# A two-block transformer-like kernel on one core: one softplus in the attention, squares on two engines, value products of four heads together, loops written out

## The reference, cut to what matters

```python
# attention: 16 heads of size 16, 1024 tokens, 4 sequences
scores = jnp.einsum('bhqd,bhkd->bhqk', q, k) * hs ** (-0.5)
p = jax.nn.softplus(scores)
p = p * p
p = p * causal
attn = p / (jnp.sum(p, axis=-1, keepdims=True) + 1e-09)
out = jnp.einsum('bhqk,bhkd->bhqd', attn, v)
...
# experts: 8, the two with the largest gate
gates = jax.nn.softmax(jnp.einsum('bsh,eh->bse', x, gate_w) + gate_b, axis=-1)
top_gates, top_idx = jax.lax.top_k(gates, TOP_K)
expert_out = jnp.einsum('bsh,eoh->bseo', x, expert_w) + expert_b
selected = jnp.take_along_axis(expert_out, top_idx[..., None], axis=2)
return (selected * top_gates[..., None]).sum(axis=2)
```

## Time and profile before

| | us |
|---|---|
| median of 3 runs | 1797.35 |
| lowest, highest | 1796.25, 1797.80 |
| span of the profiled execution, first to last instruction | 1794.8 |
| what lies around the span (median less span) | 2.55 |
| ACT busy over the whole span | 1092.9 (61%) |
| POOL busy over the whole span | 858.2 (48%) |

### The profile page before, as it was taken

How to read it: one execution, slowest core, us unless ns; L and a number is a source line. 1 busy time by engine, 2 the same in 40 slices (tenths; PEclk the granted TensorE clock), 3 DMA queues, 4 the chain that set the end, 5 groups by cost and what they waited for, 6 DMA issues and landing times. The chain is left out here.

```text
span 1794.8 us, 33269 instructions
## 1 busy us (share of the span) xinstructions
PE 1683.5 (94%) x11188; PEld 1158.1 (65%) x11188; DVE 1295.7 (72%) x2830; ACT 1092.9 (61%) x1612; POOL 858.2 (48%) x654
## 2 busy tenths in 40 slices
PE   8999897999999999998999899998899999889999
PEld 7888773333333333338788777777677777667777
DVE  5455885777777777775545788886787787778886
ACT  3332788999999999993333322214888887722120
POOL 0002108999999999995003322211265665411111
PEclk9999998999999999999999999999999999999999
DMA  5000275635535535400000100001232233200000
GB/s 164 1 0 12 91 214 90 76 48 73 68 47 73 67 47 79 62 1 1 13 1 30 29 7 0 0 0 39 83 96 95 104 112 103 95 1 24 23 23 24
DMA packets 57112, 95.09 MB, mean 53 GB/s; under 512 B 7904, under 2 KB 29632, under 8 KB 57024
## 3 DMA queue, kind: packets, MB, share of 16 engines
q1 hardware_dynamic: 56064, 93.35, 24.0%
q10 hardware_dynamic: 960, 0.59, 0.1%
HBM read 76.88 MB, written 17.04 MB: 52 GB/s over the span
## 5 line engine op out<-in xcount | busy, mean ns | idle before, releaser
L1508 POOL TENSOR_TENSOR att_weights<-att_weights 128x1024 f32<-128x1024 f32 (+1 forms) x288 | 508.9, 1799 | 9.0 <-DVE att_weights L1445 5.6
L1445 DVE SCALAR_TENSOR_TENSOR att_weights<-att_weights,ps 128x512 f32<-128x512 f32 x544 | 348.2, 684 | 145.1 <-ACT att_weights L1414 138.6
L932 DVE SCALAR_TENSOR_TENSOR X<-ps,moe_gsel,X 128x256 f32 (+1 forms) x512 | 246.6, 484 | 63.1 <-PE ps L48 44.8
L1369 PE MATMUL ps<-att_weights,att_v_ones 64*32 64x64 f32 (+5 forms) x2048 | 289.0, 399 | 1.9 <-POOL att_weights L1508 1.8
L1414 ACT ACTIVATE att_weights<-att_weights 128x1024 f32<-128x1024 f32 (+1 forms) x288 | 286.5, 1007 | 1.0
L1408 ACT ACTIVATE att_weights<-ps 128x1024 f32<-128x1024 f32 (+1 forms) x288 | 278.4, 972 | 8.6 <-PE ps L1349 7.0
L48 PE MATMUL ps<-w_experts_hi,moe_xh 128*128 128x512 f32 x512 | 205.3, 401 | 0.4 <-DVE X L932 0.4
L48 PE MATMUL ps<-w_experts_hi,moe_xl 128*128 128x512 f32 x512 | 203.2, 397 | 0.0
L48 PE MATMUL ps<-w_experts_lo,moe_xh 128*128 128x512 f32 x512 | 201.6, 394 | 0.0
L1369 PEld LDWEIGHTS ps<-att_weights,att_v_ones 128*32 128x32 f32 (+1 forms) x2048 | 82.4, 108 | 104.6 <-issue 80.2
L424 ACT ACTIVATE ffn_gates<-ps,ffn_gate_bias 128x512 f32<-128x512 f32 x72 | 49.5, 688 | 147.5 <-PE ps L48 143.2
(11 more groups left out here) (282 smaller groups left out, 3796.3 us busy)
## 6 DMA issues: line engine op xcount, KB each, us to landing
ssm_lb<-decays SPq DMA_DIRECT2D x32, 512.0 KB, 4.7
ssm_rise<-decays SPq DMA_DIRECT2D x28, 512.0 KB, 3.9
qk_parts<-qkv_part SPq DMA_DIRECT2D x32, 384.0 KB, 2.7
q_stack<-qk_parts SPq DMA_DIRECT2D x64, 128.0 KB, 4.9
k_stack<-qk_parts SPq DMA_DIRECT2D x64, 128.0 KB, 8.4
att_q_stack<-qk_parts SPq DMA_DIRECT2D x64, 128.0 KB, 4.7
att_k_stack<-qk_parts SPq DMA_DIRECT2D x64, 128.0 KB, 8.5
out<-X SPq DMA_DIRECT2D x7, 512.0 KB, 2.9
```

What stands on the lines that cost most here:

```text
L932: dve.scalar_tensor_tensor(out=x, in0=ring[:, e // 2, (e % 2) * C:(e % 2 + 1) * C], scalar=gsel[:, s, j, e:e + 1], in1=x, op0=ALU.mult, op ...
L1369: ins = pe.matmul(O(qb)[h * 2 * HD:(h + 1) * 2 * HD, q0:q0 + w], values, Wt[rows, u % WU, t, c:c + w], start=kj == 0 and part == FULL, sto ...
L1445: dve.scalar_tensor_tensor(out=wt[:, t], in0=wt[:, t], scalar=LIMIT, in1=scores(u)[:, t], op0=ALU.min, op1=ALU.max).then_inc(max_done, 2 // n)
L1508: pool.tensor_tensor(wt, wt, wt, ALU.mult).then_inc(sq_pool, 1)
```

## The change

In the attention ACT runs one `Softplus` from PSUM to SBUF in place of `Exp` and `Ln`, and DVE's min and max are gone; a score place is free when softplus has read it. The squares are split: POOL squares seven of a pass's 18 units (0, 2, 6, 8, 10, 12, 14; all wide), DVE the other eleven (nine wide, two narrow). Both operands of DVE's square lie in SBUF. The value products of a step (two units, four heads) are issued together after the second unit's square. AHEAD becomes 6 and the lags become shorter. In `choose`, `max_index` and the comparisons give way to `match_replace`: the two largest are replaced by zero in a copy, and `gsel` is half the difference. The index table and its DMA go. All `Fori` loops become Python loops, so the instructions stand written out.

```diff
-    AHEAD = 7
-    TURN_LAG, COPY_LAG, DEN_LAG, OUT_LAG = 4, 7, 9, 10
+    AHEAD = 6
+    TURN_LAG, COPY_LAG, DEN_LAG, OUT_LAG = 3, 5, 8, 9
...
+    POOL_UNITS = [u for u in range(PU) if BANKS[u] == 2 and u % 2 == 0][:7]
+    by_pool = lambda u: u % PU in POOL_UNITS
...
                 upper = segments[0][-1] == UPPER
+                pe.wait_ge(softplus_done, i * NU + u + 1)
...
-            def value_unit(i, u):
+            def value_step(i, u):
...
+                for unit in range(first, last + 1):
+                    squares_of(i, s * PU + unit)
...
-            act.preload_act_table_set(LN_EXP_SET)
+            act.preload_act_table_set(SOFTPLUS_SET)
...
-                act.activation(Wt[:, u % WU, 0:n], scores(u)[:, 0:n], ACT.Exp).then_inc(exp_done, 1)
+                act.activation(Wt[:, u % WU, 0:n], scores(u)[:, 0:n], ACT.Softplus).then_inc(softplus_done, 1)
...
-                act.activation(wt, wt, ACT.Ln, bias=1.0).then_inc(ln_done, 1)
...
-                    dve.scalar_tensor_tensor(out=wt[:, t], in0=wt[:, t], scalar=LIMIT, in1=scores(u)[:, t],
-                                             op0=ALU.min, op1=ALU.max).then_inc(max_done, 2 // n)
+                dve.wait_ge(softplus_done, SU + i * NU + u + 1)
+                wt = Wt[:, u % WU, 0:BANKS[u % PU]]
+                dve.tensor_tensor(wt, wt, wt, ALU.mult).then_inc(sq_dve, 1)
...
-                    pool.wait_ge(max_done, 2 * (SU + i * NU + u + 1))
-                    wt = Wt[:, u % WU, 0:BANKS[u % PU]]
-                    pool.tensor_tensor(wt, wt, wt, ALU.mult).then_inc(sq_pool, 1)
+                    if by_pool(u):
+                        pool.wait_ge(softplus_done, SU + i * NU + u + 1)
+                        wt = Wt[:, u % WU]
+                        pool.tensor_tensor(wt, wt, wt, ALU.mult).then_inc(sq_pool, 1)
...
+                dve.tensor_copy(taken[:, :, 0:2], best[:, :, 0:2]).then_inc(taken_done, 1)
+                dve.wait_ge(taken_done, n + 1)
                 for j in range(GT):
-                    ins = dve.max_index(place[:, j], best[:, j], prob[:, j])
...
+                    ins = dve.match_replace(rest[:, j], taken[:, j], prob[:, j], 0.0)
...
-            with pe.Fori(1, BODIES - 1) as i:
+            for i in range(1, BODIES - 1):
                 body(i)
```

More of the change, by code:

```diff
@@ L397, in _ @@
             step(0, first=True)
-            with pe.Fori(1, B - 1) as i:
+            for i in range(1, B - 1):
                 step(i)
@@ L433, in _ @@
             step(0, first=True)
-            with act.Fori(1, B - 1) as i:
+            for i in range(1, B - 1):
                 step(i)
@@ L512, in _ @@
             step(0, first=True)
-            with dve.Fori(1, B - 1) as i:
+            for i in range(1, B - 1):
                 step(i)
@@ L527, in _ @@
             norm.pool_rstd(pool, 1, 1)
-            with pool.Fori(1, GROUPS // 2) as i:
+            for i in range(1, GROUPS // 2):
                 for s in range(2):
@@ L805, in _ @@
             group(0, 0)
-            with pe.Fori(0, GROUPS // 2 - 1) as i:
+            for i in range(0, GROUPS // 2 - 1):
                 group(i * 2 + 1, 1)
@@ L868, in _ @@
             apply(1, 1)
-            with act.Fori(0, GROUPS // 2 - 1) as i:
+            for i in range(0, GROUPS // 2 - 1):
                 group(i * 2, 0)
@@ L1016, in _ @@
             split.split(pool)
-            with pool.Fori(0, GROUPS // 2 - 2) as i:
+            for i in range(0, GROUPS // 2 - 2):
                 group(i * 2, 0)
@@ L1087, in steps @@
             step(1, 0, 1, 3)
-            with eng.Fori(1, B - 2) as i:
+            for i in range(1, B - 2):
                 step(i * 2, i, 0, 3)
@@ L1213, in _ @@
             norm.pool_shift(pool, 1, 1)
-            with pool.Fori(0, GROUPS // 2 - 1) as i:
+            for i in range(0, GROUPS // 2 - 1):
                 for h in range(HALVES):
@@ L1514, in _ @@
             copy_v(0, 0, 0)
-            with pool.Fori(0, BODIES - 1) as i:
+            for i in range(0, BODIES - 1):
                 body(i)
@@ L1521, in _ @@
             load_stacks(sp, stacks, loaded, parts_dram, 0, 1, STACKED)
-            with sp.Fori(1, BODIES) as i:
+            for i in range(1, BODIES):
                 for s in range(2):
@@ L1559, in _ @@
             copy_in(0, 1)
-            with act.Fori(0, B - 1) as i:
+            for i in range(0, B - 1):
                 for h in range(HALVES):
@@ L1595, in _ @@
             project(1, 1)
-            with pe.Fori(1, GROUPS // 2 - 1) as i:
+            for i in range(1, GROUPS // 2 - 1):
                 turn_in(i * 2 + 1, 1)
@@ L1622, in _ @@
             lo(0, 0)
-            with dve.Fori(0, GROUPS // 2 - 2) as i:
+            for i in range(0, GROUPS // 2 - 2):
                 lo(i * 2 + 1, 1)
@@ L1733, in groups @@
             group(0, 0, 2)
-            with eng.Fori(0, PT // 2 - 2) as i:
+            for i in range(0, PT // 2 - 2):
                 group(i * 2 + 1, 1, 2)
@@ L2255, in _ @@
             spread(0, 0)
-            with sp.Fori(0, PT // 2 - 1) as i:
+            for i in range(0, PT // 2 - 1):
                 spread(i * 2 + 1, 1)
```

135 lines of the change are left out of this document (55 added, 80 removed).

## The result

The changed kernel takes **1651.7 us** in the median (1648.1 to 1652.8), the kernel before 1796.8 in the same session: a ratio of **0.919, 95% interval [0.918, 0.920]**, 145 us less. The prediction was 1661. The profiled execution took 1652.15 us with a span of 1650.3.

The account below looks back on a forecast made before the run. Bound now: ScalarE, GpSimd close behind; afterwards their shared VectorE-GpSimd port, 47.6 + 2, called 50 us a body. Eight bodies 400 + 9 = 409 against 541.5, with 3.5 more 136 us less: 1661 us, range 1640 to 1696 (8 in 10: 1620 to 1705).

Parts of the forecast that it names:

- ACT: ScalarE in an attention body: one softplus per unit, assumed to cost what `Exp` costs, 32 us.
- A dear softplus: Rival: attention slower than before because softplus is expensive; at 3.0 us a wide unit 2070 us in all; chance 0.03.
- PE: TensorE in an attention body: scores, value products, transposes, 41 us; as rival limit 1589 us in all, wholly or partly 0.12.
- unjoined heads: Rival in the attention's value products: four heads not running together, 56 us a body, 1709 us; 0.10 shared with dearer hand-overs.
- DVE and POOL alone: Attention body, each engine's own work without hindrance: VectorE 29 us, GpSimd 28 us.
- The port: VectorE's two-SBUF-input squares and GpSimd's instructions exclude each other in the attention: 47.6 us a body; chance 0.75 (47.6 to 54).
- The gaps: Attention body: 2 us added because the port won't be full, making 49.6, called 50 us; bounds 47.6 and 54.
- Start, end, clock: Attention outside its eight bodies: 6 us for start and end, 3 us for the half clock (bounds 0 and 8).
- The rest: Savings beside the attention's main sum: expert picking -0.5 us and written-out loops -3 us, together 3.5 us.
- Loops alone: Written-out loops: 0.2 us per group in the state-space layer, -3 us for all stages (bounds -6 and +3).
- the picking: `choose`, picking the experts: a few instructions fewer, hidden behind TensorE except in the first group, -0.5 us.
- Signs: New profile: VectorE's wide squares about 2 us, GpSimd's above 1.89, TensorE waiting for `att_oT` or squares, ScalarE below 70% busy.

Follow-up runs that it names:

- Four kernels that take the port away or relieve it: Against the changed kernel: VectorE squares all, 1607.5 us; VectorE reads one input from PSUM, 1607.2; ScalarE takes three VectorE units, 1603.3; ScalarE four, GpSimd none, 1589.6.

## Why the prediction was right, step by step

- **ACT.** 32 us a body from `Exp`'s row; measured 170.39 / 5 = 34.1 busy with overlapping ends, mean 0.976 us. A dear softplus is excluded.
- **PE.** 41 us from single steps; measured 41.3 where nothing else holds it (the kernel in which ScalarE and VectorE square), and 58.2 with unjoined heads where the prediction had 56. The 0.99 us for four heads came exactly, and the narrow products of four column tiles still start within 0.02 us of each other:

```profile
440.29 0.23 PE L1382 MATMUL ps<-att_weights,att_v_ones 64*32 64x64 f32 x1
440.30 0.23 PE L1382 MATMUL ps<-att_weights,att_v_ones_up 64*32 64x64 f32 x1
440.31 0.23 PE L1382 MATMUL ps<-att_weights,att_v_ones 64*32 64x64 f32 x1
440.31 0.22 PE L1382 MATMUL ps<-att_weights,att_v_ones_up 64*32 64x64 f32 x1
```

- **DVE and POOL alone.** 29 and 28 us: with one input in PSUM DVE is busy 29.7 us a body and POOL 28.4.
- **The port.** The step that carried the forecast. 1.09 us was read from the state-space layer with an estimated end of GpSimd's instruction, and 1.74 was 1.89 less 0.15, for which no row was given; measured here 1.07, 1.08 and 1.76. Four kernels that take the port away or relieve it fall to 43.7, 44.5 (42.5 at best), 43.1 and 41.3 us a body. Here the Trainium skill ("SBUF — State Buffer", section "SBUF: two separate sides") says that whichever of the two starts first has the pair for the whole instruction. The ends in the timeline agree; the last section has a case where squares that started later than GpSimd's copy went ahead of it, which that rule doesn't give.
- **The gaps.** 2 us over the port's 47.6 were taken, 49.1 - 47.6 = 1.5 came. The forecast went by 50 us, 0.9 above the measured body: 0.5 of that is the guess and 0.4 the rounding of 49.6. 8 x 0.9 = 7.2 us of the 9 us by which the forecast was too high. The 2 us were a guess and not a sum; that they came out so near is partly luck.
- **Start, end, clock.** 9 us taken (6 and 3), 400.3 - 8 x 49.1 = 7.5 came, and the trace doesn't part the two. The granted clock is near half for two short whiles (0.53 over 273.4 to 280.3 us and over 293.9 to 300.8 us). The first body, at 0.89, is still the shortest of the seven (47.9 us), but its lists are shorter too (492 matmuls, the later ones about 571), so it doesn't show that the half clock cost nothing. The first score's wait for the table load, 1.3 us, wasn't in the sum.
- **The rest.** -3.5 taken, -3.3 came, but not as split, and partly by luck: the -3.3 us lie outside the attention, while the -3.5 were meant for all stages. Loops alone give about 5 us for the whole program (forecast 3), 1.9 of them in the attention (541.5 to 539.7 us in that kernel's profile), and the picking 1.8 us in M (forecast 0.5), which isn't seen in the total. "Each of M, S and F less than 1 us shorter" was wrong for M.
- **Signs.** Squares of 2.03 (wide alone: 2.04) and 2.45 us, PE waiting for `att_oT`, ACT at 69%: all as said.

## What to carry to other kernels

When work moves from an engine that reads PSUM to one that reads SBUF twice, add up VectorE's and GpSimd's pieces as if they were one engine; a second engine that is slower per piece (1.74 against 1.09 us) makes the pair slower than VectorE alone. Here taking GpSimd's squares away altogether won 44 us, and giving some of VectorE's to ScalarE, which had time left and squares a wide unit in 1.05 us, 18 more. And before cutting a wait of TensorE, ask who is late: here moving the consumer of a late result further back only moved the wait.

## What the runs showed of the hardware beyond that

The exclusion holds for GpSimd's plain copies too, and it isn't always by turns. With VectorE squaring everything, GpSimd's copies of V (0.61 and 0.40 us when free) last 2.1 and 3.7 us. Timelines of that kernel:

```profile
368.48 2.12 POOL L1488 COPY att_v_ones<-v 128x512 f32<-128x512 f32 x1 [15.94 <-PE ps L1382]
370.65 3.73 POOL L1490 COPY att_v_ones_up<-v 64x256 f32<-64x256 f32 x1
```

```profile
370.63 3.48 DVE L1435 TENSOR_TENSOR att_weights<-att_weights 128x1024 f32<-128x1024 f32 x3
374.04 0.17 DVE L1447 TENSOR_SCALAR att_den<-ps 128x16 f32<-128x16 f32 x1
```

The second copy starts at 370.65 and ends at 374.38, 0.27 us behind three squares that ran from 370.63 to 374.11 without a break, each at its usual length. VectorE kept the port through back-to-back squares; GpSimd came in when an instruction on PSUM followed. It isn't that a copy always has to wait so: in the kernel with three units on GpSimd the same copy stands right behind a GpSimd square and gets in between two squares of VectorE:

```profile
425.60 2.15 POOL L1498 TENSOR_TENSOR att_weights<-att_weights 128x1024 f32<-128x1024 f32 x1 [3.02 <-ACT att_weights L1419]
427.70 1.60 POOL L1488 COPY att_v_ones<-v 128x512 f32<-128x512 f32 x1
...
426.53 3.86 DVE L1435 TENSOR_TENSOR att_weights<-att_weights 128x1024 f32<-128x1024 f32 x2
```

GpSimd's square ends at 427.75 and its copy at 429.30; VectorE's pair ends at 430.39, 1.09 us behind the copy, so its second square ran after the copy and its first between 427.75 and about 428.84. In the changed kernel, where both engines hold long squares, they alternate too. What decides between the two patterns wasn't tried.
